# Results of the first layer's routed blocks added to a table of tokens by one indirect accumulating DMA per block

## What is computed

```python
x = x + jnp.tanh(g_xattn[0]) * _L0_xattn_ref(_layernorm(x, axis=-1), ctx_1024, ...)
x = x + jnp.tanh(g_ffn[0]) * _L0_ffn_ref(_layernorm(x, axis=-1), ...)
x = x + jnp.tanh(g_xattn[1]) * _L1_xattn_ref(_layernorm(x, axis=-1), ctx_1024, ...)
x = x + jnp.tanh(g_ffn[1]) * _L1_ffn_ref(_layernorm(x, axis=-1), ...)

def _L0_ffn_ref(x, router_w, rms_w, w1, w2, rms_w_s, w1_s, w2_s):
    gates = jax.nn.softmax(xf @ router_w, axis=-1)
    top_v, top_i = jax.lax.top_k(gates, TOP_K)
    masked = jnp.zeros_like(gates).at[jnp.arange(N)[:, None], top_i].set(top_v)
    masked = masked / (masked.sum(axis=-1, keepdims=True) + EPS)
    routed = jax.vmap(lambda rw_, W1_, W2_: _ffn(xf, rw_, W1_, W2_))(rms_w, w1, w2)
    routed_out = jnp.einsum('end,ne->nd', routed, masked)
    shared = jax.vmap(lambda rw_, W1_, W2_: _ffn(xf, rw_, W1_, W2_))(rms_w_s, w1_s, w2_s).sum(0)
    return (routed_out + shared).reshape(B, T, D)
```

## Time and profile before

| | value |
|---|---|
| profiled execution, its own time | 1200.99 us |
| its span, first to last instruction | 1199.4 us |
| PE busy | 868.5 us, 72% |
| DVE busy | 674.6 us, 56% |
| ACT busy | 491.5 us, 41% |
| POOL busy | 335.8 us, 28% |
| granted TensorE clock, mean | 0.884 |
| DMA traffic | 85.18 MB, mean 71 GB/s |

### The profile page before, as it was taken

One profiled execution on the slowest core, in us unless ns is written; L12 is line 12 of the kernel. 1 busy time (PEld: TensorE's weight loads), 2 busy tenths in 40 slices (PEclk: granted clock), 3 DMA queues, 4 the chain that ended last, 5 costly groups with the idle time before them and its releaser, 6 DMA issues. The chain is left out here.

```text
span 1199.4 us, 23482 instructions
## 1 busy us (share of the span) xinstructions
PE 868.5 (72%) x7667; PEld 682.1 (57%) x7667; DVE 674.6 (56%) x1559; ACT 491.5 (41%) x1049; POOL 335.8 (28%) x342
## 2 busy tenths in 40 slices
PE   2302799999987375547999998376785789889970
PEld 1101576767656364537877776366673566666650
DVE  5600677777765889714434333376773555555548
ACT  2101365556653423201233232154663566666650
POOL 0012333333310326770000000485761222222220
PEclk9855799999999577767999999698897999999995
DMA  2376222222210335630122221477320000000002
GB/s 61 92 169 204 63 67 66 67 65 65 54 22 1 107 131 150 195 92 26 32 72 63 70 65 54 130 201 205 116 74 0 1 0 1 0 1 0 0 1 61
DMA packets 84904, 85.18 MB, mean 71 GB/s; under 512 B 23718, under 2 KB 76118, under 8 KB 84822
## 3 DMA queue, kind: packets, MB, share of 16 engines
q1 hardware_dynamic: 77574, 71.47, 21.2%
q0 software_dynamic: 6144, 11.96, 4.0%
q10 hardware_dynamic: 1104, 0.64, 0.2%
HBM read 52.90 MB, written 16.25 MB: 58 GB/s over the span
## 5 line engine op out<-in xcount | busy, mean ns | idle before, releaser
L615 DVE TENSOR_REDUCE a_mx<-ps 112x2 f32<-112x750 f32 x128 | 119.8, 936 | 43.9 <-PE ps L508 40.0
L1939 POOL TENSOR_TENSOR f_rl<-f_rf,f_rh 128x448 bf16<-128x448 f32 x64 | 66.2, 1035 | 185.9 <-DVE f_rh L1967 185.9
L51 PE MATMUL ps<-f_w2hi,f_hh 128*128 (+1 forms) x292 | 85.0, 291 | 36.2 <-DVE f_hl L1293 29.5
L1291 DVE CAST f_hh<-f_hf 128x512 bf16<-128x512 f32 (+1 forms) x57 | 29.4, 516 | 133.4 <-ACT f_hf L1153 84.2
L579 ACT ACTIVATE a_Pf<-ps 125x672 f32<-125x672 f32 x128 | 89.7, 729 | 12.8 <-PE ps L456 11.9
L1447 POOL DMA_INDIRECT a_yg<-f_yd,pos x32 | 32.7, 1023 | 216.6 <-POOLq L88 208.2
L1920 ACT ACTIVATE f_rf<-ps,f_ln 128x112 f32<-128x112 f32 x256 | 91.7, 436 | 0.9 <-PE ps L1896 0.9
L51 PE MATMUL ps<-f_w2hi,f_hl 128*128 (+1 forms) x292 | 84.6, 290 | 4.9 <-issue 4.9
L51 PE MATMUL ps<-f_w2lo,f_hh 128*128 (+1 forms) x292 | 84.4, 289 | 4.3 <-issue 4.3
L51 PE MATMUL ps<-f_w2hi,f_rh 128*112 128x256 bf16 x256 | 73.2, 286 | 19.6 <-POOL f_rl L1939 19.6
L51 PE MATMUL ps<-f_xgThi,f_w1hi 128*128 128x128 bf16 x328 | 73.8, 227 | 7.7 <-issue 5.5
(11 more groups left out here) (351 smaller groups left out, 2572.2 us busy)
## 6 DMA issues: line engine op xcount, KB each, us to landing
f_raw<-F_w SPq DMA_DIRECT2D x28, 512.0 KB, 5.0
a_ctxF<-ctxT SPq DMA_DIRECT2D x16, 375.0 KB, 3.2
a_cT<-ctxT SPq DMA_DIRECT2D x16, 375.0 KB
a_cR<-ctx SPq DMA_DIRECT2D x16, 375.0 KB
a_stkQ<-a_QS SPq DMA_DIRECT2D x48, 112.0 KB, 2.3
f_xd<-a_zero SPq DMA_DIRECT2D x1, 5248.0 KB, 18.2
f_xg<-f_xd SPq DMA_DIRECT2D x41, 128.0 KB
f_yd<-f_yo SPq DMA_DIRECT2D x41, 128.0 KB, 1.7
```

The source lines that it names most:

```text
L51: ins = nc.tensor.matmul(out, l, r, start=first and i == 0, stop=last and i == len(steps) - 1)
L615: nc.vector.reduce_max(mx[:, n.odd, 2 * j:2 * j + 2], psMX[:T, :, :S], AX).then_inc(mx_red, 1)
L1291: nc.vector.tensor_copy(hh[:, s.odd, 0:n], hf[:, 0:n]).then_inc(h_hi, 1)
L1939: nc.gpsimd.tensor_tensor(rl[:, t.odd], rf[:, t.odd], rh[:, t.odd], ALU.subtract).then_inc(r_lo, 1)
```

## The change

The table `xd` gets two more columns in each row (`ROW` = D + 2 = 258): the token's index (an integer) and its gate. The zero fill writes these too, with an index behind the last token for rows that no token takes. The 16 scatters of the first choice carry the first gate; then DVE overwrites the gate column at step 13 (`GATE_AT` = 2 * SH - 3, SH being 8), after the first 16 scatters have landed, and the other 16 scatters follow.

A new table in DRAM, `xa`, has one row for each token. SP stores `xs` to it in four groups (`base`), each once the shared units have added to it. One DMA reads the two columns of all 41 blocks into the tile `ig` (128 x 41 x 2). ACT multiplies a block's result by the gate column while it writes `yo`. POOL then adds the 128 rows of `yo` to the rows of `xa` that the index column names, by one indirect accumulating DMA for each block, and waits for each before it issues the next. The table `yd`, its 41 stores, the 32 gathers, the tile `yg` and the two multiply-adds of `front` go; instead SP loads `xs` from `xa`, two sequences at a time.

```diff
-        self.xn = self.sb("xn", [T, B, D], F32)
+        self.xn_row = self.sb("xn", [T, B, ROW], F32)
+        self.xn = self.xn_row[:, :, 0:D]
...
@@ l0_attention, sync
-                sp.wait_ge(zero_set, 1)
+                sp.wait_ge(zero_set, 2)
                 sp.dma_start(xd.rearrange("(n p) d -> p n d", p=P),
-                             zero[:].unsqueeze(1).broadcast_to([P, NBLK, D])).then_inc(k.filled, 16)
+                             zero[:].unsqueeze(1).broadcast_to([P, NBLK, ROW])).then_inc(k.filled, 16)
+                sp.dma_start(xa[N:N + P], zero[:, 0:D]).then_inc(k.filled, 16)
...
@@ l0_experts, sync
                 for l in LOADS:
                     load(l)
+                def base(g):
+                    sp.wait_ge(ys_used, B + GB * (g + 1))
+                    sp.dma_start(xa[g * GT:(g + 1) * GT].rearrange("(b t) d -> t b d", t=T), k.xs[:, GB * g:GB * (g + 1), :]).then_inc(xa_in, 16)
+
+                for g in range(NG - 1):
+                    base(g)
                 sp.wait_ge(scattered, 16 * 2 * B)
-                for b in range(NBLK + XG_AHEAD):
-                    if b < NBLK:
-                        if b >= 3:
-                            sp.wait_ge(t_full, b - 2)
-                        sp.dma_start(xg[:, b % 3, :], xd[b * P:(b + 1) * P, :]).then_inc(xg_in[b % 3], 16)
-                    d = b - XG_AHEAD
-                    if d >= 0:
-                        sp.wait_ge(y_out, d + 1)
-                        sp.dma_start(yd[d * P:(d + 1) * P, :], yo[:, d % 3, :]).then_inc(y_st[d % 3], 16)
...
+                for b in range(NBLK):
+                    if b >= 3:
+                        sp.wait_ge(t_full, b - 2)
+                    sp.dma_start(xg[:, b % 3, :], xd[b * P:(b + 1) * P, 0:D]).then_inc(xg_in[b % 3], 16)
+                    if b == 1:
+                        base(NG - 1)
+                        sp.dma_start(ig[:], xd.rearrange("(n p) d -> p n d", p=P)[:, :, D:ROW]).then_inc(ig_in, 16)
@@ l0_experts, gpsimd
                 for i in range(2):
+                    pool.wait_ge(gate_set, i + 1)
                     for b in range(B):
                         nc.gpsimd.indirect_dma_start(
                             out=xd, out_offset=bass.IndirectOffsetOnAxis(pos[:, i, b:b + 1], 0),
-                            in_=k.xn[:, b, :], in_offset=None, bounds_check=NBLK * P - 1, oob_is_err=True).then_inc(scattered, 16)
-
-                pool.wait_ge(scattered, 16 * 2 * B)
+                            in_=k.xn_row[:, b, :], in_offset=None, bounds_check=NBLK * P - 1, oob_is_err=True).then_inc(scattered, 16)
+
+                pool.wait_ge(ig_in, 16)
+                pool.wait_ge(xa_in, 16 * NG)
+                for b in range(NBLK):
+                    pool.wait_ge(y_out, b + 1)
+                    if b:
+                        pool.wait_ge(y_add, 16 * b)
+                    nc.gpsimd.indirect_dma_start(
+                        out=xa, out_offset=bass.IndirectOffsetOnAxis(ig[:, b, 0:1].bitcast(I32), 0), in_=yo[:, b % 3, :],
+                        in_offset=None, bounds_check=N + P - 1, oob_is_err=True, compute_op=ALU.add).then_inc(y_add, 16)
+                pool.wait_ge(y_add, 16 * NBLK)
@@ l0_experts, scalar
                 def out(s):
                     act.wait_ge(y_full, s.u + 1)
+                    if s.block == 0:
+                        act.wait_ge(ig_in, 16)
                     if s.block >= 3:
-                        act.wait_ge(y_st[s.block % 3], 16 * (s.block // 3))
-                    nc.scalar.activation(yo[:, s.block % 3, :], k.ps[:, 4 + s.odd, 0:D], ACT.Copy).then_inc(y_out, 1)
+                        act.wait_ge(y_add, 16 * (s.block - 2))
+                    nc.scalar.activation(yo[:, s.block % 3, :], k.ps[:, 4 + s.odd, 0:D], ACT.Copy,
+                                         scale=ig[:, s.block, 1:2]).then_inc(y_out, 1)
@@ l0_experts, vector
+                    if s == GATE_AT:
+                        dve.wait_ge(scattered, 16 * B)
+                        nc.vector.tensor_copy(k.xn_row[:, :, D + 1], gate[:, 1, :]).then_inc(gate_set, 1)
...
@@ l1_attention, sync
+                def rows(p):
+                    sp.dma_start(k.xs[:, two(p)], xa[cols(p)].rearrange("(b t) d -> t b d", t=T)).then_inc(xs_in[p], 16)
+
+                rows(0)
...
                 for b in range(B):
+                    if b < 4:
+                        rows(2 * b + 1)
+                        if b < 3:
+                            rows(2 * b + 2)
                     load(b)
@@ l1_attention, vector
                 def front(b):
-                    dve.wait_ge(yg_in[b], 32)
-                    stt(k.xs[:, b, :], yg[:, 0, b, :], k.gate[:, 0, b:b + 1], k.xs[:, b, :], ALU.mult, ALU.add).then_inc(add_done, 1)
-                    dve.wait_ge(add_done, 2 * b + 1)
-                    stt(k.xs[:, b, :], yg[:, 1, b, :], k.gate[:, 1, b:b + 1], k.xs[:, b, :], ALU.mult, ALU.add).then_inc(add_done, 1)
-                    dve.wait_ge(add_done, 2 * b + 2)
+                    dve.wait_ge(xs_in[b // 2], 16)
                     nc.vector.bn_stats(stats[:, b, :], k.xs[:, b, :]).then_inc(st_done, 1)
```

More of the change, by code:

```diff
@@ L17 @@
 U32 = mybir.dt.uint32
+I32 = mybir.dt.int32
 P = 128
@@ L34 @@
 L0_GATE_EPS, L1_GATE_EPS = 1e-9, 1e-8
+ROW = D + 2
 NBLK = (2 * N - E0 - (2 * N - E0) % P) // P + E0
@@ L369, in l0_attention @@
         attn = k.xn
-        zero = sb("zero", [P, D], F32)
+        zero = sb("zero", [P, ROW], F32)
         ONES = 200
@@ L589, in _ @@
                 nc.gpsimd.memset(zero[:], 0.0).then_inc(zero_set, 1)
+                pool.wait_ge(zero_set, 1)
+                nc.gpsimd.iota(zero[:, D:D + 1].bitcast(I32), pattern=[[0, 1]], base=N, channel_multiplier=1).then_inc(zero_set, 1)
                 nc.gpsimd.memset(V[:], 0.0).then_inc(v_zero, 1)
@@ L927, in l0_experts @@
         xg_in = [sem(f"xgin{i}") for i in range(3)]
-        y_st = [sem(f"yst{i}") for i in range(3)]
+        ig = sb("ig", [P, NBLK, 2], F32)
+        ig_in, xa_in, y_add, gate_set, rows_set = sem("igin"), sem("xain"), sem("yadd"), sem("gateset"), sem("rowsset")
         (rw_in, r_in, made, tri_done, w1_hi, w1_lo, w2_hi, w2_lo, eps_set, st_done, var_done, root_done, step, xn_dve,
@@ L942, in l0_experts @@
         RANK_AT = 3
+        GATE_AT = 2 * SH - 3
         XG_AHEAD = 3
@@ L975, in _ @@
                     load(l)
-                sp.wait_ge(scattered, 16 * 2 * B)
-                for b in range(NBLK + XG_AHEAD):
-                    if b < NBLK:
-                        if b >= 3:
-                            sp.wait_ge(t_full, b - 2)
-                        sp.dma_start(xg[:, b % 3, :], xd[b * P:(b + 1) * P, :]).then_inc(xg_in[b % 3], 16)
-                    d = b - XG_AHEAD
-                    if d >= 0:
-                        sp.wait_ge(y_out, d + 1)
-                        sp.dma_start(yd[d * P:(d + 1) * P, :], yo[:, d % 3, :]).then_inc(y_st[d % 3], 16)
-                for i in range(3):
-                    sp.wait_ge(y_st[i], 16 * len(range(i, NBLK, 3)))
+                def base(g):
[3 more added lines that the diff above has]
+                    base(g)
+                sp.wait_ge(scattered, 16 * 2 * B)
+                for b in range(NBLK):
[5 more added lines that the diff above has]
+                        sp.dma_start(ig[:], xd.rearrange("(n p) d -> p n d", p=P)[:, :, D:ROW]).then_inc(ig_in, 16)
             @block.gpsimd
@@ L993, in _ @@
                 nc.gpsimd.iota(iota_i[:, 2 * E:], pattern=[[1, NBLK]], base=0, channel_multiplier=0).then_inc(made, 1)
+                nc.gpsimd.iota(k.xn_row[:, :, D].bitcast(I32), pattern=[[T, B]], base=0, channel_multiplier=1).then_inc(rows_set, 1)
                 nc.gpsimd.memset(tri[:], 1.0).then_inc(tri_done, 1)
@@ L1260, in choose @@
                     link(tt(gate[:, 1, :], gate[:, 0, :], top[:, 1, :], ALU.mult))
+                    nc.vector.tensor_copy(k.xn_row[:, :, D + 1], gate[:, 0, :]).then_inc(gate_set, 1)
                 def place():
@@ L1389, in l1_attention @@
         wv_in = sem("wvin")
-        yg_in = [sem(f"ygin{b}") for b in range(B)]
+        xs_in = [sem(f"xsin{p}") for p in range(NP)]
         cT_in = [sem(f"ctin{i}") for i in range(CT)]
@@ L1444, in _ @@
             def _(pool):
-                def gather(b):
-                    for i in range(2):
-                        nc.gpsimd.indirect_dma_start(
-                            out=yg[:, i, b, :], out_offset=None, in_=yd,
-                            in_offset=bass.IndirectOffsetOnAxis(k.pos[:, i, b:b + 1], 0),
-                            bounds_check=NBLK * P - 1, oob_is_err=True).then_inc(yg_in[b], 16)
-                gather(0)
                 nc.gpsimd.memset(half[:], -0.5).then_inc(half_set, 1)
@@ L1455, in _ @@
                 for i in range(FIRST, LAST):
-                    if batch(i + 7):
-                        gather(i + 7)
                     if i % 2 == 0 and pair((i + 4) // 2):
```

24 lines of the change are left out of this document (12 added, 12 removed).

## The result

The changed kernel took 1238.01 us (median of 4 runs, 1235.16 to 1240.19) beside 1200.93 us of the kernel before on the same chip: a ratio of 1.030, 95% interval 1.025 to 1.036. The profiled execution spans 1235.3 us, 35.9 more than the 1199.4 of before.

The account below looks back on a forecast made before the run. PE was taken to set the pace of the routed blocks, 4.00 us each. The terms 2 + 3 + 14 + 35 - 8 = +46 on 1199.5 us gave 1246 us, range 1206 to 1320 us.

Parts of the forecast that it names:

- the likeliest case: Routed blocks: the serial adding DMAs set a period of 4.2 to 5.6 us; chance 0.52.
- The fill: Zero fill of `xd` with rows of 1032 instead of 1024 bytes, nothing covering it: +2 us (0.1 to 4.6).
- The second half of the scatters: Sixteen scatters held until the gate copy; PE may be slow again beside them: +3 us (-3 to +8).
- The fourth base and `ig`: SP issues both ahead of the third `xg`, which comes 12.4 us late with nothing covering it: +14 us (+9 to +23).
- the prediction's own sign: The prediction is wrong if the chain's period is outside 4.2 to 5.6 us, or `ig` lands in a few us.
- The chain: Routed blocks: 41 serial adding DMAs at 4.8 us each, 196.8 us against 161.6: +35 us (+2 to +80).
- The second attention: Gathers and DVE work go, eight loads of 224 KB come, gains overlap: -8 us (-3 to -18).
- Rival A: Routed blocks: the chain is hidden, period under 4.00 us; +13, 1212 us; chance 0.20.
- Rival B: Routed blocks: adding in the DMA is slow as well, period 6.5 us; +116, 1316 us; chance 0.17.
- Rival C: Routed blocks: PE is slowed beside every indirect DMA, about +90 on a 4.8 us chain; 1336 us; chance 0.06.
- Rival D: Second attention gives all it could, -27, with the chain hidden and other terms low: -16, 1184 us; chance 0.05.

Follow-up runs that it names:

- the plain: The changed kernel with the 41 indirect DMAs writing their rows instead of adding them, every wait kept: 1206.71 us, ratio 1.019.
- two-table version: The changed kernel with even and odd blocks added to two tables, so two adding DMAs may be in flight: 1218.85 us, ratio 1.028.
- 258-float kernel: The kernel before with rows of 258 floats in the table of dispatched rows and nothing else of the change: 1184.3 us, ratio 0.999.
- early load: The changed kernel with the third `xg` ahead of the `ig` load and the fourth base behind the fifth `xg`: 1230.79 us (1.037), repeated 1226.56 us (1.0345).

## Why the prediction was right, and where its sizes were off

It said 1246 us and slower; 1238 was measured, and the likeliest case, a chain period between 4.2 and 5.6 us, is the one that came. The chip had a part in how near it came: the change costs 37 us on the first chip and 51 on the fourth, and the sum of 46 lies between. By its steps:

**The fill, +2.** Landing after 20.1 us for 18.2, and ACT's first context 2.6 us later: right. Seven later traces with the wide rows have 20.2 to 22.5 us, all five with narrow rows 18.2 or 18.3, so that +2 to +4 is the term. The Trainium skill (DMA: Bandwidth & Descriptors, How a descriptor splits into AXI transactions) gave an estimate of +4.5: its direction agrees, and its size is just over the largest that was measured, +4.3. By its rule the fifth transaction comes with the 8 bytes left over, wherever a row starts, and not only from the uneven start that the prediction named.

**The second half of the scatters, +3.** The first transposes were put near 574 and came at 574.49. Part of that is luck, since the four traces without the split on the chips with the slow stretch have block 0's transposes anywhere from 568.5 to 582.2. The reason was half wrong. PE was not slow again beside the second sixteen: from 554 to 570 it executed nothing, because block 0's transposes, which need the last scatter, stand in its order ahead of the products of units 14 and 15 (unit 14's add comes at 580.79). And what made the last scatter late is the place of the gate's copy, not the first sixteen's landing: the sixteenth was issued at 526.99 and landed near 529.6 (with the 2.56 us of the earlier trace rows), but DVE's copy stands at step 13 and ran at 548.64 without a wait in front, so POOL sat idle for 21.4 us, and for 14.6 to 17.3 in the seven other traces with the split. What an earlier step would give, no run measured. The term holds only where the kernel before pays PE's slow stretch itself. There the split trades one loss for the other (ratio 1.002 when made alone). Where that stretch is absent, the split costs 16.5 and 17.6 us: on the second chip the plain and the two-table version have 62.7 and 63.8 us from the first scatter to block 0's transposes, the 258-float kernel 46.2. That fits the same kernel being at 1.030 on one chip and at 1.040 on another. The kernel before was not traced on the fast chips; that it lacks the slow stretch there rests on the 258-float kernel, which had its time within 0.3%.

**The fourth base and `ig`, +14.** Right place, size 11.8 from block 0 to the first `yo`. `ig` landed in 6.0 us, not in 10.0 and more: the price of 30.4 ns a run from the earlier trace rows was too high for runs of 8 bytes. By the prediction's own sign (wrong if `ig` lands in a few us) this term was near failing. One row was read wrongly too: in the earlier trace rows the transposes at 586.43 are those of block 3; block 2's were at 583.50. So the third `xg` was 9.8 us late (593.30), not the 12.4 of the text. The early load took 9.9 us of the 11.8 away. The rest comes with the split: made alone it has 13.7 us from block 0's transposes to the first `yo` (574.10 to 587.76) instead of 12.0, with PE at a granted clock of 0.50 from 570 to 575 us after its pause.

**The chain, +35.** Measured 4.71 us a DMA for 4.8, and +31.7. The period was right though its parts were not, and that is luck. POOL's issue is 1.54 us, not the gather's 1.0; all in, landing takes 3.8 us, less than the 4.8 of read and write one after the other; and the 0.9 us of POOL's reaction had no term. The waits in the trace bear the mechanism out: ACT waits 90.1 us before `yo` for `f_xa` (28 times), and before it had waited for PE alone. The scale was not free, 0.47 us a `yo` for 0.38, which ACT's idle time hides. Rival A needed c below 4.00: it is what the plain indirect DMA does (3.92, with PE setting it), so the addition decides the case. The Trainium skill's fit (DMA: Bandwidth & Descriptors, Anatomy of one DMA), an estimate of 2.3 us for the DMA, agrees with the plain write, landed in 2.4, and not with the adding one. Rival B's 6.5 us did not occur. Rival C did not either: PE's 150.56 us for 1481 matmuls are those of the earlier trace rows, while each block has an indirect DMA beside it.

**The second attention, -8.** It gave 14.1 us. The term took 8.4 us for the loads and nearly nothing for the engines. Without gathers and multiply-adds the stage is 21.5 us shorter, and with adding gathers in place of the multiply-adds, which load POOL with 16 us more, it is not shorter at all. The gain came with the gathers and multiply-adds together; how it divides between DVE's time, POOL's time and the transfers, no run separates. Rival D's -27 was beyond what the stage could give.

**What had no term: the end of the stage, +5.9.** The sum priced the last landing but not what follows. From there to the next stage's first instruction there were 1.6 us before, where POOL had long been done and SP's store came last. Where POOL is last there are 4.3 us behind a mere wait of POOL's, 4.4 behind one DMA of its own, and 7.4 to 7.6 behind forty-one with POOL's wait (five traces, one with plain DMAs); with SP waiting in its place, 5.1. So a late POOL accounts for a part without any DMA, and the addition for none of it; why it is 3 us more in the kernels with forty-one is open.

Measured less predicted, in us: ahead of block 0's transposes 0.3 - 5 = -4.7, at `ig` 11.8 - 14 = -2.2, the chain -3.3, the attention -6.1, and the missing term +5.9. Together -10, for a sum of 36 instead of 46: the errors partly cancelled, and the forecast was closer than its terms. The -4.7 is within what two executions differ by at this place.

Open are the cause of PE's slow stretch beside the scatters, and why it is missing in every trace from the other two chips. In the trace of before PE waited there for nothing that the profile shows:

```profile
PE ps L51 <- issue: 22.5, 14, 3.7
```

That is 22.5 us in 14 waits, the longest 3.7 us, which lies just ahead of 519; the other 18.8 us lie between 519 and 547. What POOL does in the time before it leaves a stage is open as well.

## What to carry to other kernels

Here a serial chain of DMAs beside a pipeline cost nothing while its period, with the waiting engine's reaction and issue in it, stayed under the pipeline's 4.0 us, and the whole difference times the count above it. So price the period of the actual operation (adding 4.7 us, plain at most 3.9) before moving a sum into DRAM. Two destinations hid the chain, but the reader pays for both (8 to 16 us), and a load that only a later step needs must not be queued ahead of one that is needed now. When an edit holds work back for a signal, put the signal where its data are ready: here it came 19 us after them, because of its place in an engine's program. A saving seen against one chip's baseline may be a loss that this chip happens to have: if a term rests on an unexplained slow stretch, keep a second value for the case that it is not there.

## What the runs showed of the hardware that was not expected

- An indirect DMA that adds takes POOL 1.54 us to issue against 0.97 for the same one that writes, and lands after 3.8 instead of 2.4 us. Whether it writes into DRAM (1545 ns) or gathers into SBUF (1514 ns) makes little difference to POOL.
- The issue of a DMA right behind the fill of 5289 KB held SP's queue for 12.18 us (11.25 behind the fill of 5248 KB before the change).
- A load of 5248 runs of 8 bytes landed in 5.9 to 6.0 us with a store of 448 KB issued just ahead of it (four traces), and in 4.9 to 5.1 without (three).
- The next stage starts 4.3 to 4.4 us after POOL is done if POOL is last, with or without a DMA of its own, and 7.4 to 7.6 us after it in the kernels with forty-one indirect DMAs in the stage, against 1.6 us behind SP's last store.
- The kernel before took 1184 to 1187 us on two chips and 1201 to 1205 on two others, while the changed kernel took 1236 and 1238.
